# Cross attention with its value products issued once per group of four heads, and the second query tile's transposed scores divided by heads

## The chip, the core and the metric

The kernel runs on one core of one Trainium2 chip. The metric is the device time of one execution, in microseconds (us). The runs of the kernel before took 505.22, 505.7 and 510.95 us (median 505.7). The execution that the profiler recorded took 508.26 us, with a span of 506.4 us between its first and last instruction.

## What is computed

Four batches of 256 tokens with 256 channels pass through a gated cross attention and then a gated transformer block (self attention with 16 heads of 128, then four experts). The change touches only the cross attention, which in the reference is, for 16 query heads of 16 channels and 4 key/value heads:

```python
q = _rms_norm(q, q_norm_w)          # q: 256 tokens x 256
k = _rms_norm(k, k_norm_w)          # k, v: 256 tokens x 64
# heads, then rotary position on q and k
qg = q.reshape(B, N_KV_HEADS, g, T, hd)         # 4 groups of g = 4 heads
scores = jnp.einsum('bgnqd,bgkd->bgnqk', qg, k) * scale
scores = jnp.where(causal, scores, -1e+30)
attn = jax.nn.softmax(scores, axis=-1)
out = jnp.einsum('bgnqk,bgkd->bgnqd', attn, v)
return out.reshape(B, T, C) @ w_out.T
```

## The kernel before

**Cross attention.** A batch has 256 queries in two tiles of 128 and 256 keys in two tiles of 128. Work goes by group `m` of four heads that share one key head: 4 batches x 4 groups = 16 groups. Each group has three pieces, and piece `p = 3m + z` runs through a software pipeline of 53 steps (`for p in range(NPX + VLAG)`, with NPX = 48 and VLAG = 5). `k` is the step's number within a batch, 0 to 11. In step `p` TensorE does, in this order:

- `x_scores(p)` (L1102, matmuls L1112 and L1113): scores with queries on the partitions, in one of two PSUM banks `S_B`. It waits for `s_max` of piece p-2. VectorE takes the row maxima of them in `x_max` (L801, L810) into `nxm`.
- in some steps `q_turn` (L1069, eight transposes; ScalarE copies them out in `q_evac`, L477), `out_turn` (L1079) and `out_project` (L1090).
- `x_turned(p - 3)` (L1116): the same scores again with keys on the partitions, in a bank of `PT_B`, 512 columns a piece. Piece z = 0 is key tile 0 with query tile 0, z = 1 is key tile 0 with query tile 1, z = 2 is key tile 1 with query tile 1, each for all four heads. L1126 is the product, L1128 adds the causal mask where key and query tile are the same, and L1130 subtracts each head's row maximum by a matmul of 128 columns per head ("shift matmul": a column of `nxm` broadcast as weights, times the identity). ScalarE turns a piece into probabilities in `x_exp` (L495, L500), in one of four slots of `probs`.
- in some steps `norm_turn` (L1093, L1099), transposes of normed rows `nh` that VectorE makes in `residual` (L748, phases 0 to 5 in six steps, `nh` at L780).
- in steps p = 9, 12, ... `o_turn` (L1149, L1155), which transposes the group's outputs. VectorE divides them by the softmax sums in `norm_out` (L734, L742 and L744).
- `x_values(p - 5)` (L1134, L1145): probabilities times values, four matmuls of 128x32 weights, one for each head, each on 32 partitions of `bank[4]`. They take float32, and the trace has two records for each matmul. ScalarE copies the group's result to `oT` in `oT_evac` (L488, L493) after the third piece.

Each engine runs its instructions in the order in which they are written here. VectorE's step holds `x_max(p)`, then what the step has of `norm_q`, `hidden_t`, `norm_out`, `pack` (L707, copies L711 to L715) and `residual`. GpSimd makes the next batch's queries in `prep` (L319), then splits weights (L377 to L385), then `hidden_low` (L387). There are no loads from DRAM in the pipeline except two weight loads that SyncE starts near its end.

**After it** come a short stage that starts the self attention (`project_qk` and `project_v`, all at L1192), the self attention's loop, and the experts. Their code is the same in both kernels. The last `norm_turn` before them is that of batch 2 (L1184), and TensorE can't pass it before VectorE has written `nh`.

Of the kernel before, what the change touches and what calls it, by code (L numbers as in the profile page):

```python
# [12 lines left out]
ACT = mybir.ActivationFunctionType  # L13
AX = mybir.AxisListType

P = 128
# [4 lines left out]
XH, XG, XD = 16, 4, 16  # L21
XS = 8
XP = 12
VP = 32
TLAG, VLAG = 3, 5
# [22 lines left out]
def build_kernel(nc, x, ctx_in, cst, cols, rows, bv, wqkv, wo, w_out_t, w_gate, be2, we, out):  # L48
    with ExitStack() as stack:
        def sb(name, shape, dt=F32):  # L50
            return stack.enter_context(nc.sbuf_tensor(name, shape, dt))
# [45 lines left out]
        sm = sb("sm", [P, 2, 384])  # L97
        nm = sb("nm", [P, 2, 2])
        rs = sb("rs", [P, 2, 2])
        probs = sb("probs", [P, 4, 512])  # L100
        PR = probs[:, 0:2, :]
        PTs = probs[:, 2:4, :]
        o_parts = sb("o_parts", [P, 2, 1024], F32R)
# [21 lines left out]
        kT = yacc[:, :, :].rearrange("p t n -> p (t n)").bitcast(BF16).rearrange("p (b g n) -> p b g n", b=B, g=XG)  # L125
        qT = qk_room[:, :, :].rearrange("p a n -> p (a n)").bitcast(BF16).rearrange("p (x t h n) -> p x t h n", x=2, t=2, h=8)


        v_slots = room[:, 0:NT * XG * VP].rearrange("p (n d) -> p n d", d=VP)
# [6 lines left out]
        nxm = sb("nxm", [P, 3, 8], BF16)  # L136
# [11 lines left out]
        bank = [ps(f"bank{n}") for n in range(8)]  # L148
        S_B = bank[0:2]
        PT_B = bank[2:4]  # L150
# [4 lines left out]
        ident_bf = bf_sb[:, 0:P]  # L155
        mask_bf = bf_sb[:, P:2 * P]
# [9 lines left out]
        s = {n: sem(n) for n in names.split()}  # L166
# [11 lines left out]
            g, j = divmod(k, 3)  # L178
            return (g, 0, [4 * g + n for n in range(4)]) if j == 0 else (g, 1, [4 * g + 2 * (j - 1) + n for n in range(2)])

        def block_of(z):

            return ((0, 0), (0, 1), (1, 1))[z]


        M6, M7 = [("Q", 0, 0, 0), ("Q", 0, 0, 1)], [("K", b) for b in range(B)]
        for b in range(B):
# [274 lines left out]
        def _(act):  # L462
# [24 lines left out]

            def oT_evac(m):  # L488

                act.wait_ge(s["pv_pe"], 3 * m + 3)  # L490
                if m >= 2:
                    act.wait_ge(s["o_pe"], m - 1)
                act.activation(oT[:, m % 2, :], bank[4][:, 0:256], ACT.Copy).then_inc(s["oT_ready"], 1)  # L493

            def x_exp(p):  # L495

                act.wait_ge(s["st_pe"], p + 1)
                if p >= 4:
                    act.wait_ge(s["pv_pe"], p - 3)
                act.activation(probs[:, p % 4, :], PT_B[p % 2][:, :], ACT.Exp).then_inc(s["s_exp"], 1)  # L500

            q_evac(0, 0, 0)
            q_evac(0, 0, 1)
            for p in range(NPX + VLAG):
                b, k = divmod(p, XP)
# [92 lines left out]
            for n in range(2 * NE):  # L598
# [8 lines left out]
                c, m = divmod(n, NE)  # L607
# [439 lines left out]
        def _(pe):  # L1047
# [68 lines left out]
            def x_turned(p):  # L1116

                b, k = divmod(p, XP)
                m, z = divmod(p, 3)
                g, h = k // 3, 4 * (k // 3)  # L1120
                kt, t = block_of(z)
                pe.wait_ge(s["s_max"], 3 * m + (1 if z == 0 else 3))
                if p >= 2:
                    pe.wait_ge(s["s_exp"], p - 1)
                by_head = PT_B[p % 2][:, :].rearrange("p (h n) -> p h n", h=4)
                pe.matmul(by_head, kT[:, b, g, kt * P:(kt + 1) * P], qT[:, h // 8, t, h % 8:h % 8 + 4, :], start=True, stop=False)  # L1126
                if kt == t:
                    pe.matmul(by_head, mask_bf, ident_bf.unsqueeze(1).to_broadcast([P, 4, P]), start=False, stop=False)  # L1128
                for n in range(4):
                    ins = pe.matmul(PT_B[p % 2][:, n * P:(n + 1) * P], nxm[:, m % 3, 4 * t + n:4 * t + n + 1].to_broadcast([P, P]), ident_bf,  # L1130
                                    start=False, stop=(n == 3))
                ins.then_inc(s["st_pe"], 1)

            def x_values(p):  # L1134

                b, k = divmod(p, XP)
                m, z = divmod(p, 3)
                kt, t = block_of(z)
                pe.wait_ge(s["s_exp"], p + 1)
                if p == 0:  # L1140
                    pe.wait_ge(s["va_ready"], 1 + B)
                if z == 0 and m:
                    pe.wait_ge(s["oT_ready"], m)
                for n in range(4):
                    ins = pe.matmul(bank[4][32 * n:32 * (n + 1), t * P:(t + 1) * P], v_slots[:, XG * (2 * b + kt) + k // 3, :],  # L1145
                                    probs[:, p % 4, n * P:(n + 1) * P], start=(z != 2), stop=(z != 1))
                ins.then_inc(s["pv_pe"], 1)

            def o_turn(m):  # L1149
# [14 lines left out]
            for p in range(NPX + VLAG):  # L1164
                b, k = divmod(p, XP)
                if p < NPX:
                    x_scores(p)
                    if k in (3, 4):
                        q_turn(b, 1, k - 3)
                    if k == 8 and b:  # L1170
                        out_turn(b - 1)
                    if k == 9 and b:
                        out_project(b - 1)
                    if k in (9, 10) and b + 1 < B:
                        q_turn(b + 1, 0, k - 9)
                if TLAG <= p < NPX + TLAG:
                    x_turned(p - TLAG)
                if k == 5 and b >= 2:
                    norm_turn(b - 2)
                if p >= 9 and p % 3 == 0:  # L1180
                    o_turn((p - 9) // 3)
                if p >= VLAG:
                    x_values(p - VLAG)
            norm_turn(B - 2)  # L1184

            def three(outp, pairs):
# [260 lines left out]
```

## Time and profile before

| | before |
|---|---|
| runs | 505.22, 505.7, 510.95 us |
| profiled execution | 508.26 us, span 506.4 us |
| TensorE matmuls | 453.2 us busy, 89% of the span |
| VectorE | 367.1 us, 72% |
| ScalarE | 239.6 us, 47% |
| GpSimd | 232.8 us, 46% |

"PE" is TensorE's matmuls and "PEld" its weight loads, which overlap them. DVE is VectorE, ACT ScalarE, POOL GpSimd. Matmuls are pipelined, so a matmul's own duration (0.2 us and more) is longer than the time after which the next starts. What a matmul costs in a full stream is read from the distance between starts. The cross attention's pipeline lies from about 30 to 125 us of the span.

### The profile page before, as it was taken

How to read it: one execution, taken by the hardware profiler on the slowest of the kernel's cores; microseconds unless marked ns; L12 is line 12 of the kernel's file. 1: busy time of each engine (PE TensorE's matmuls, PEld its weight loads, DVE VectorE, ACT ScalarE, POOL GpSimd, SP SyncE). 2: the span in 40 equal slices, each digit the busy share in tenths (PEclk: the TensorE clock that was granted, in tenths of full speed). 3: DMA queues.
4: the chain of work that ended last, by engine and by line, in shares of the span. 5: the costliest groups of instructions: out<-in, count | busy, mean ns of one | idle time of the engine just before them, and what ended most of it. 6: DMA issues, size and time to landing. Idle time of an engine off the chain costs nothing.

```text
span 506.4 us, 10710 instructions
## 1 busy us (share of the span) xinstructions
PE 453.2 (89%) x3396; PEld 386.2 (76%) x3396; DVE 367.1 (72%) x1163; ACT 239.6 (47%) x613; POOL 232.8 (46%) x318
## 2 busy tenths in 40 slices
PE   0289998898777999999999999999999998689996
PEld 0166666675565899999999999999999997578895
DVE  5876669776557878788788887887877878835544
ACT  2026555453113555555655546556455565164342
POOL 5945709710345545446446445346454431162342
PEclk9999999999979999999999999999999998897899
DMA  8100000200123343352342532532533310000011
GB/s 286 28 3 1 2 1 3 84 1 1 23 62 84 72 119 84 84 145 64 78 133 58 143 85 62 145 74 52 144 83 83 77 29 0 2 0 2 0 43 42
DMA packets 19881, 31.41 MB, mean 62 GB/s; under 512 B 6020, under 2 KB 8200, under 8 KB 19848
## 3 DMA queue, kind: packets, MB, share of 16 engines
q1 hardware_dynamic: 15928, 22.31, 18.1%
q10 hardware_dynamic: 3920, 8.69, 5.7%
q8 instruction: 18, 0.29, 0.2%
q14 instruction: 15, 0.12, 0.1%
HBM read 13.16 MB, written 1.05 MB: 28 GB/s over the span
## 4 chain that ended last, share of the span: by engine, by line
PE 80%; DVE 12%; POOL 3%; issue 3%; DMA 1%; ACT 1%; ACTq 0%; DVEq 0%
PE bank L1192 42%; PE bank L1272 5%; PE bank L1235 5%; PE bank L1263 4%; PE bank L1145 3%; PE bank L1112 3%; PE bank L1273 3%; PE bank L1234 3%; PE bank L1126 2%; PE bank L1130 2%; PE bank L1090 1%; PE bank L1113 1%; PE bank L1128 1%; PE bank L1069 1%; DMA rows_sb<-in_rows 1%
## 5 line engine op out<-in xcount | busy, mean ns | idle before, releaser
L401 POOL TENSOR_TENSOR room<-room,qk_room 128x512 f32<-128x512 f32 x64 | 82.3, 1287 | 102.8 <-DMA qk_room<-qk_room 102.6
L542 ACT ACTIVATE probs<-sm,nm 128x128 f32<-128x128 f32 (+1 forms) x128 | 57.3, 448 | 116.2 <-DVE nm L917 116.2
L1192 PE MATMUL bank<-hH,qk_parts 128*128 128x512 f32 x256 | 81.0, 398 | 0.0
L840 DVE SCALAR_TENSOR_TENSOR qk_room<-bank,qk_bias,cst_sb 128x512 f32<-128x512 f32 x64 | 48.0, 750 | 37.2 <-PE bank L1192 35.8
L1192 PE MATMUL bank<-hL,qk_parts 128*128 128x512 f32 x128 | 62.4, 488 | 6.6 <-DVE room L840 5.7
L1192 PEld LDWEIGHTS bank<-hH,qk_parts 128*128 128x128 f32 x256 | 48.8, 191 | 10.1
L840 DVE SCALAR_TENSOR_TENSOR room<-bank,qk_bias,cst_sb 128x512 f32<-128x512 f32 x64 | 47.6, 743 | 0.0
L1192 PE MATMUL bank<-woH,o_parts 128*128 128x256 f32 x256 | 47.2, 283 | 0.0
L810 DVE TENSOR_REDUCE nxm<-bank 128x2 bf16<-128x512 f32 (+1 forms) x48 | 32.5, 688 | 14.9 <-PE bank L1113 14.3
L500 ACT ACTIVATE probs<-bank 128x512 f32<-128x512 f32 x48 | 28.6, 596 | 26.1 <-PE bank L1130 25.4
L1192 PE MATMUL bank<-woL,o_parts 128*128 128x256 f32 x128 | 39.0, 305 | 1.1 <-DVE o_parts L905 1.1
L1192 PEld LDWEIGHTS bank<-woH,o_parts 128*128 128x128 f32 x256 | 40.0, 192 | 0.0
L1272 PE MATMUL bank<-probs,V 128*128 128x256 f32 x128 | 39.0, 387 | 0.6 <-DVE o_parts L905 0.6
L1192 PE MATMUL bank<-wvL,hH 128*128 128x256 f32 x128 | 39.3, 307 | 0.0
L1235 PE MATMUL bank<-room 128*128 128x256 f32 x128 | 38.2, 380 | 0.0
L1192 PE MATMUL bank<-wvH,hH 128*128 128x256 f32 x128 | 36.4, 284 | 0.0
L450 POOL TENSOR_TENSOR qk_parts<-G,o_parts 128x512 fp32r<-128x512 f32 x16 | 20.7, 1298 | 34.0 <-ACT o_parts L616 33.5
L1192 PE MATMUL bank<-wvH,hL 128*128 128x256 f32 x128 | 36.3, 283 | 0.0
L1263 PE MATMUL bank<-cst_sb,probs 128*128 128x128 f32 x192 | 31.7, 274 | 4.9 <-DVE probs L961 4.9
L351 POOL TENSOR_TENSOR qk_parts<-stg,qk_parts 128x256 fp32r<-128x256 f32 x32 | 23.8, 743 | 26.5 <-ACT qk_parts L566 26.5
L556 ACT ACTIVATE o_parts<-bank,bv_pair 128x256 fp32r<-128x256 f32 x64 | 30.3, 474 | 11.6 <-PE bank L1273 10.8
L1263 PEld LDWEIGHTS bank<-cst_sb,probs 128*128 128x128 f32 x192 | 24.4, 140 | 14.6 <-DVE probs L961 6.8
(200 smaller groups left out, 1242.2 us busy)
## 6 DMA issues: line engine op xcount, KB each, us to landing
qk_room<-qk_room SPq DMA_DIRECT2D x128, 128.0 KB, 2.3
stg<-in_wqkv ACTq DMA_DIRECT2D x6, 768.0 KB, 4.6
stge<-in_we ACTq DMA_DIRECT2D x7, 256.0 KB, 3.2
stg<-in_wqkv SPq DMA_DIRECT2D x2, 768.0 KB, 6.4
stgo<-in_wo ACTq DMA_DIRECT2D x6, 256.0 KB, 3.6
x_sb<-in_x SPq DMA_DIRECT2D x4, 256.0 KB, 6.2
out_y<-yacc SPq DMA_DIRECT2D x4, 256.0 KB, 2.3
cst_sb<-in_cst SPq DMA_DIRECT2D x1, 520.0 KB, 6.9
```

What stands on the lines that cost most here:

```text
L351: pool.tensor_tensor(wqkL[:, c], stg[:, k, :, r * HD:(r + 1) * HD], wqkH[:, c].bitcast(F32), ALU.subtract).then_inc(s["wqk_ready"], 1)
L401: pool.tensor_tensor(v, v, qk_sw[:, q, :], ALU.subtract).then_inc(s["rope_done"], 1)
L450: pool.tensor_tensor(GL[:, (n // 2) % 2, n % 2, :], G[:, n % 2, :], GH[:, (n // 2) % 2, n % 2, :].bitcast(F32), ALU.subtract).then_inc(s[" ...
L500: act.activation(probs[:, p % 4, :], PT_B[p % 2][:, :], ACT.Exp).then_inc(s["s_exp"], 1)
L542: ins = act.activation(PR[:, q, a:e], sm[:, q, a:e], ACT.Exp, bias=nm[:, q, t:t + 1], scale=-1.0, accum_out=rs[:, q, t:t + 1])
L556: act.activation(oH[:, ((j - 2) // 2) % 2, q, :], bank[3][:, 0:256], ACT.Identity, bias=head_bias(j)).then_inc(s["b_oH"], 1)
L810: dve.tensor_reduce(nxm[:, m % 3, a:a + len(heads)], S_B[p % 2][:, :].rearrange("p (h n) -> p h n", h=len(heads)), AX.X, ALU.max, negate=T ...
L840: return dve.scalar_tensor_tensor(out.rearrange("p (b t) -> p b t", b=2), O_B[q][:, :].rearrange("p (b t) -> p b t", b=2), qk_bias[:, c:c ...
L1192: ins = pe.matmul(outp, l, r, start=(m == 0), stop=(m == n - 1))
L1235: pe.matmul(S_B[j % 2][:, P:3 * P], QT[:, 2 * r, second], QT[:, 2 * r + 1, both], start=True, stop=True).then_inc(s["b_s"], 1)
L1263: ins = pe.transpose(bank[2][:, n * P:(n + 1) * P], PR[:, 1 - q, n * P:(n + 1) * P], ident)
L1272: pe.matmul(bank[3][:, 0:256], V[:, 2 * b, r * HD:(r + 1) * HD], PTs[:, q, 0:256], start=True, stop=False)
```

## The change

The code of three functions and the storage of the probabilities change.

- `x_values` is called once per group, in steps p = 7, 10, 13, ... (`x_values((p - 7) // 3)`), and issues all twelve matmuls there. Before, four were issued in every step from p = 5. The group's third set of four was in the same step as the twelve are now. Its wait for the copy `oT_ready` of the group before moves with it, two steps later than before. `pv_pe` counts groups now, and `oT_evac` and `x_exp` wait accordingly.
- `probs` has six slots instead of four, three for each of two groups. `x_exp` waits for the values of two groups before.
- For the second query tile `x_turned` puts heads 0 and 1 with both key tiles into piece z = 1, heads 2 and 3 with both key tiles into piece z = 2. The product is two matmuls of 256 columns, the mask one of 256 columns, and a head's shift is one matmul of 2x128 columns that serves both key tiles. The columns of a group add up to 4096 before and after.

The core of the diff:

```diff
-        probs = sb("probs", [P, 4, 512])
+        probs = sb("probs", [P, 6, 512])
...
+        def prob_slot(m, z):
+
+            return probs[:, 3 * (m % 2) + z, :]
...
-                act.wait_ge(s["pv_pe"], 3 * m + 3)
+                act.wait_ge(s["pv_pe"], m + 1)
...
+                m, z = divmod(p, 3)
                 act.wait_ge(s["st_pe"], p + 1)
-                if p >= 4:
-                    act.wait_ge(s["pv_pe"], p - 3)
-                act.activation(probs[:, p % 4, :], PT_B[p % 2][:, :], ACT.Exp).then_inc(s["s_exp"], 1)
+                if m >= 2:
+                    act.wait_ge(s["pv_pe"], m - 1)
+                act.activation(prob_slot(m, z), PT_B[p % 2][:, :], ACT.Exp).then_inc(s["s_exp"], 1)
...
-                pe.wait_ge(s["s_max"], 3 * m + (1 if z == 0 else 3))
+                pe.wait_ge(s["s_max"], p + 1)
...
+                else:
+                    by_keys = PT_B[p % 2][:, :].rearrange("p (k h n) -> p k h n", k=2, h=2)
+                    first = 2 * (z - 1)
+                    for kt in range(2):
+                        pe.matmul(by_keys[:, kt, :, :], kT[:, b, g, kt * P:(kt + 1) * P],
+                                  qT[:, h // 8, 1, h % 8 + first:h % 8 + first + 2, :], start=(kt == 0), stop=False)
+                    pe.matmul(by_keys[:, 1, :, :], mask_bf, ident_bf.unsqueeze(1).to_broadcast([P, 2, P]), start=False, stop=False)
+                    for n in range(2):
+                        ins = pe.matmul(by_keys[:, :, n, :], nxm[:, m % 3, 4 + first + n:5 + first + n].to_broadcast([P, P]),
+                                        ident_bf.unsqueeze(1).to_broadcast([P, 2, P]), start=False, stop=(n == 1))
...
-                if z == 0 and m:
+                else:
                     pe.wait_ge(s["oT_ready"], m)
-                for n in range(4):
-                    ins = pe.matmul(bank[4][32 * n:32 * (n + 1), t * P:(t + 1) * P], v_slots[:, XG * (2 * b + kt) + k // 3, :],
-                                    probs[:, p % 4, n * P:(n + 1) * P], start=(z != 2), stop=(z != 1))
+                for kt, t in ((0, 0), (0, 1), (1, 1)):
+                    for n in range(4):
+                        z, c = (0, n) if t == 0 else (1 + n // 2, 2 * kt + n % 2)
+                        ins = pe.matmul(bank[4][32 * n:32 * (n + 1), t * P:(t + 1) * P], v_slots[:, XG * (2 * b + kt) + g, :],
+                                        prob_slot(m, z)[:, c * P:(c + 1) * P], start=(kt == 0), stop=(kt == t))
...
-                if p >= VLAG:
-                    x_values(p - VLAG)
+                if p >= 7 and p % 3 == 1:
+                    x_values((p - 7) // 3)
```

TensorE's order in step 22 (k = 10 of batch 1), from the second `q_turn` of that pair to the first scores of step 23. L1145 is the value product, L1126 and L1130 the transposed scores and their shift. Before:

```order
L1069 MATMUL bank<-bf_sb,q_room 128x128 [waits m6_free,qpack_ready]
L1069 MATMUL bank<-bf_sb,q_room 128x128 x7
L1126 MATMUL bank<-qk_room,yacc 128x512 [waits s_exp,s_max]
L1130 MATMUL bank<-bf_sb,nxm 128x128 x4
L1145 MATMUL bank<-probs,room 32x128 [waits s_exp]
L1145 MATMUL bank<-probs,room 32x128 x3
L1112 MATMUL bank<-yacc,qk_room 128x256 [waits s_max,m6_free]
```

The same place of the change, where the value product is L1153 and the second tile's transposed scores L1134 to L1138:

```order
L1069 MATMUL bank<-bf_sb,q_room 128x128 [waits m6_free,qpack_ready]
L1069 MATMUL bank<-bf_sb,q_room 128x128 x7
L1134 MATMUL bank<-qk_room,yacc 128x256 [waits s_exp,s_max]
L1134 MATMUL bank<-qk_room,yacc 128x256
L1136 MATMUL bank<-bf_sb 128x256
L1138 MATMUL bank<-bf_sb,nxm 128x2x128 x2
L1153 MATMUL bank<-probs,room 32x128 [waits oT_ready,s_exp]
L1153 MATMUL bank<-probs,room 32x128 x11
L1112 MATMUL bank<-yacc,qk_room 128x256 [waits s_max,m6_free]
```

Twelve value products stand where four stood, and the wait for `oT_ready` is here now.

TensorE's order in step 23, the next one. Before:

```order
L1126 MATMUL bank<-qk_room,yacc 128x512 [waits s_exp,s_max]
L1128 MATMUL bank<-bf_sb 128x512
L1130 MATMUL bank<-bf_sb,nxm 128x128 x4
L1145 MATMUL bank<-probs,room 32x128 [waits oT_ready,s_exp]
L1145 MATMUL bank<-probs,room 32x128 x3
L1112 MATMUL bank<-yacc,qk_room 128x128 [waits s_max,m7_free,m6_free]
```

The change:

```order
L1134 MATMUL bank<-qk_room,yacc 128x256 [waits s_exp,s_max]
L1134 MATMUL bank<-qk_room,yacc 128x256
L1136 MATMUL bank<-bf_sb 128x256
L1138 MATMUL bank<-bf_sb,nxm 128x2x128 x2
L1112 MATMUL bank<-yacc,qk_room 128x128 [waits s_max,m7_free,m6_free]
```

No value product and no wait for `oT_ready` is left in this step, nor in step 24 behind `o_turn`.

## Rows read from the trace of the kernel before

**Rows 1.** Page, part 1: busy us, share of the span, instructions.
```profile
PE 453.2 (89%) x3396; PEld 386.2 (76%) x3396; DVE 367.1 (72%) x1163; ACT 239.6 (47%) x613; POOL 232.8 (46%) x318
```
**Rows 2.** By stretch: length, busy us of PE, PEld, DVE, ACT, POOL; clock, DMA.
```profile
43.00:70.00 27.00, 26.83 (x353) 18.64 (x352) 15.76 (x38) 15.61 (x26) 12.18 (x26) 1.00 0.01 2
70.26:83.40 13.14, 11.69 (x156) 7.76 (x155) 12.59 (x39) 7.12 (x13) 7.15 (x17) 1.00 0.01 1
83.40:95.10 11.70, 11.59 (x137) 8.18 (x135) 7.96 (x20) 6.42 (x12) 11.12 (x22) 1.00 0.06 12
95.10:107.40 12.30, 10.69 (x146) 7.18 (x146) 11.78 (x36) 6.52 (x11) 2.79 (x3) 1.00 0.22 79
107.40:116.40 9.00, 9.00 (x104) 6.39 (x101) 4.57 (x12) 3.67 (x7) 2.50 (x2) 1.00 0.00 0
```
**Rows 3.** Timeline of TensorE, steps 24 to 26: start us, us, instruction, count.
```profile
72.21 0.39 PE L1130 MATMUL bank<-bf_sb,nxm 128*128 128x128 bf16 x4
72.43 0.39 PE L1155 MATMUL bank<-cst_sb,V 128*128 128x128 f32 x2
...
75.11 0.39 PE L1130 MATMUL bank<-bf_sb,nxm 128*128 128x128 bf16 x4
75.43 0.43 PE L1145 MATMUL bank<-probs,room 128*32 128x128 f32 x8
75.79 0.23 PE L1112 MATMUL bank<-yacc,qk_room 128*128 128x128 bf16 x1
```
**Rows 4.** Timeline of TensorE at the end of the pipeline.
```profile
122.34 0.64 PE L1145 MATMUL bank<-probs,room 128*32 128x128 f32 x16
124.98 0.66 PE L1099 MATMUL bank<-cst_sb,nh 128*128 128x128 f32 x4 [2.00 <-DVE nh L780]
```
**Rows 5.** Timeline of ScalarE and TensorE, steps 21 to 23.
```profile
66.91 1.02 ACT L477 ACTIVATE qk_room<-bank 128x1024 bf16<-128x1024 bf16 x1 [2.54 <-PE bank L1069]
68.38 0.61 PE L1069 MATMUL bank<-bf_sb,q_room 128*128 128x128 bf16 x8
70.43 0.39 ACT L493 ACTIVATE V<-bank 128x256 f32<-128x256 f32 x1
70.49 0.39 PE L1130 MATMUL bank<-bf_sb,nxm 128*128 128x128 bf16 x4
70.96 0.43 PE L1145 MATMUL bank<-probs,room 128*32 128x128 f32 x8
```
**Rows 6.** Timeline of VectorE: idle time and its releaser in brackets.
```profile
70.26 0.69 DVE L810 TENSOR_REDUCE nxm<-bank 128x2 bf16<-128x512 f32 x1 [0.33 <-PE bank L1113]
...
83.83 0.69 DVE L810 TENSOR_REDUCE nxm<-bank 128x4 bf16<-128x512 f32 x1 [0.46 <-PE bank L1113]
...
95.44 1.31 DVE L712 COPY q_room<-q_room 128x256 bf16<-128x256 bf16 x1
...
108.10 0.69 DVE L810 TENSOR_REDUCE nxm<-bank 128x4 bf16<-128x512 f32 x1 [0.70 <-PE bank L1113]
```
**Rows 7.** TensorE's waits for VectorE within the pipeline.
```profile
82.22 0.66 PE L1099 MATMUL bank<-cst_sb,nh 128*128 128x128 f32 x4 [1.37 <-DVE nh L780]
...
100.06 0.27 PE L1112 MATMUL bank<-yacc,qk_room 128*128 128x256 bf16 x1 [1.51 <-DVE nxm L810]
```
**Rows 8.** Timeline of GpSimd: start and end of its chain.
```profile
75.66 0.73 POOL L329 TENSOR_TENSOR G<-qn,WC 128x256 f32<-128x256 f32 x1 [11.53 <-DVE qn L681]
...
96.61 1.28 POOL L394 TENSOR_TENSOR yacc<-yacc,rows_sb 128x512 f32<-128x512 f32 x1
```
**Rows 9.** Timeline of TensorE behind the pipeline: its longest waits.
```profile
135.18 0.50 PE L1192 MATMUL bank<-hL,qk_parts 128*128 128x512 f32 x1 [2.12 <-DVE room L840]
...
141.08 0.79 PE L1192 MATMUL bank<-hL,qk_parts 128*128 128x512 f32 x1 [2.81 <-DVE room L840]
```
**Rows 10.** Busy us by stretch behind the pipeline, columns as in rows 2.
```profile
142.00:144.00 2.00, 2.00 (x6) 1.41 (x6) 0.00 (x0) 0.00 (x0) 0.61 (x1) 0.50 0.35 79
...
146.00:148.00 2.00, 1.31 (x7) 1.11 (x6) 2.00 (x5) 1.23 (x2) 1.24 (x2) 0.74 0.05 11
```

More of the change, by code:

```diff
@@ L179, in piece @@
             return (g, 0, [4 * g + n for n in range(4)]) if j == 0 else (g, 1, [4 * g + 2 * (j - 1) + n for n in range(2)])
-        def block_of(z):
-            return ((0, 0), (0, 1), (1, 1))[z]
+        def prob_slot(m, z):
+            return probs[:, 3 * (m % 2) + z, :]
         M6, M7 = [("Q", 0, 0, 0), ("Q", 0, 0, 1)], [("K", b) for b in range(B)]
@@ L1120, in x_turned @@
                 g, h = k // 3, 4 * (k // 3)
-                kt, t = block_of(z)
-                pe.wait_ge(s["s_max"], 3 * m + (1 if z == 0 else 3))
+                pe.wait_ge(s["s_max"], p + 1)
                 if p >= 2:
                     pe.wait_ge(s["s_exp"], p - 1)
-                by_head = PT_B[p % 2][:, :].rearrange("p (h n) -> p h n", h=4)
-                pe.matmul(by_head, kT[:, b, g, kt * P:(kt + 1) * P], qT[:, h // 8, t, h % 8:h % 8 + 4, :], start=True, stop=False)
-                if kt == t:
+                if z == 0:
+                    by_head = PT_B[p % 2][:, :].rearrange("p (h n) -> p h n", h=4)
+                    pe.matmul(by_head, kT[:, b, g, 0:P], qT[:, h // 8, 0, h % 8:h % 8 + 4, :], start=True, stop=False)
@@ L1128, in x_turned @@
                     pe.matmul(by_head, mask_bf, ident_bf.unsqueeze(1).to_broadcast([P, 4, P]), start=False, stop=False)
-                for n in range(4):
-                    ins = pe.matmul(PT_B[p % 2][:, n * P:(n + 1) * P], nxm[:, m % 3, 4 * t + n:4 * t + n + 1].to_broadcast([P, P]), ident_bf,
-                                    start=False, stop=(n == 3))
-                ins.then_inc(s["st_pe"], 1)
[L1134 to L1140, printed above, removed]
+                    for n in range(4):
+                        ins = pe.matmul(by_head[:, n, :], nxm[:, m % 3, n:n + 1].to_broadcast([P, P]), ident_bf, start=False, stop=(n == 3))
+                else:
[8 more added lines that the diff above has]
+                                        ident_bf.unsqueeze(1).to_broadcast([P, 2, P]), start=False, stop=(n == 1))
@@ L1141, in x_values @@
+                ins.then_inc(s["st_pe"], 1)
+            def x_values(m):
+                b, g = divmod(m, XG)
+                pe.wait_ge(s["s_exp"], 3 * m + 3)
+                if m == 0:
                     pe.wait_ge(s["va_ready"], 1 + B)
-                if z == 0 and m:
+                else:
                     pe.wait_ge(s["oT_ready"], m)
-                for n in range(4):
-                    ins = pe.matmul(bank[4][32 * n:32 * (n + 1), t * P:(t + 1) * P], v_slots[:, XG * (2 * b + kt) + k // 3, :],
-                                    probs[:, p % 4, n * P:(n + 1) * P], start=(z != 2), stop=(z != 1))
+                for kt, t in ((0, 0), (0, 1), (1, 1)):
+                    for n in range(4):
+                        z, c = (0, n) if t == 0 else (1 + n // 2, 2 * kt + n % 2)
+                        ins = pe.matmul(bank[4][32 * n:32 * (n + 1), t * P:(t + 1) * P], v_slots[:, XG * (2 * b + kt) + g, :],
+                                        prob_slot(m, z)[:, c * P:(c + 1) * P], start=(kt == 0), stop=(kt == t))
```

## The prediction

> **What bounds the kernel now.** The page's busy times come first [rows 1]: TensorE has 89% of the span, the next engine 72%. Only the cross attention's pipeline changes, about 30 to 125 us, so I read that part by stretches [rows 2]. The reader should see two kinds. From 43 to 70 us and from 107.4 to 116.4 us TensorE is busy 26.8 of 27.0 and 9.0 of 9.0 us, with VectorE at 58% and 51%: there TensorE sets the pace. From 70.3 to 83.4 and from 95.1 to 107.4 us VectorE is busy 12.6 of 13.1 and 11.8 of 12.3 us, and TensorE has gaps. Then VectorE sets the pace. The timeline of TensorE shows those gaps [rows 7]: 1.37 us at 82.22 for `nh` (step 29) and 1.51 us at 100.06 for a row maximum (step 38). What TensorE saves in a stretch of the second kind makes such a gap longer, and nothing else.
>
> **The value products.** A set of four costs more than its matmuls, because the array changes from 128-column to 32-column weights and back. Four shift matmuls take 0.22 us when something with full width follows (72.21 to 72.43), but L1145 starts 0.32 us after them (75.11 to 75.43), and full width resumes 0.36 us after that (75.79) [rows 3]. So a set takes 0.10 + 0.36 = 0.46 us; the printed starts are rounded, and I take 0.455. The profile has one place with two sets back to back [rows 4]: 16 records in 0.64 us, against 8 records in 0.43 us [rows 3]. A further set behind the first costs 0.21 to 0.22 us. Twelve products in a row then cost 0.455 + 2 x 0.215 = 0.885 us, where three sets cost 1.365 us. That saves 0.48 us a group, and with starts printed to 0.01 us it may be 0.46 to 0.50. I use 0.47, so 16 x 0.47 = 7.5 us of TensorE time in all.
>
> The bounds of that: if the switch went away and nothing else did, the saving would be two times (0.10 + 0.36 - 0.215), the same 0.49. If a run of twelve behaved like three separate sets, it would be 0. The back-to-back row is the same operation with the same operands, so I stay by it.
>
> The Trainium skill (TensorE: Matmul & The Clock Gate, the section on packing small matmuls) states that a weight load overlaps running matmuls only when it goes to another row group. All twelve products use all rows, so by that rule they would not overlap. The row with 16 records does not agree with it.
>
> **The transposed scores.** The columns stay 4096 a group. Two products of 256 columns stand for one of 512, and four shifts of 2x128 for eight of 128; matmuls per group go from 17 to 16 there. Starts follow each other by columns: 128 columns take 0.055 us (four in 0.22 [rows 3]). I take the sum as nothing. A fixed cost of some ns a matmul would change it by under 0.02 us a group either way, 0.3 us in all; nothing in the trace has the two-part 2x128 output, and if it wrote at half rate the four shifts would cost 0.43 us more a group, 7 us in all. The existing scores and mask matmuls already read the identity repeatedly over heads and run at full rate, so I give that little weight. The earlier wait (`s_max` of p rather than of the whole group) gains nothing: two pieces later has been reduced before `x_scores` of the same step could pass.
>
> **Waits that move.** In step 23 L1145 waits for `oT_ready` [rows 5]: the shifts end their slot at 70.71, the switch would allow 70.81, it starts at 70.96, because ScalarE's copy L493 ran until 70.82. That is 0.15 us, in steps 11, 17, 23 and 35, where ScalarE is late by its 1.02 us `q_evac`. The change asks for that copy two steps later, so this goes. But the value set between the two `q_turn` of a pair goes too. The second one starts at 68.38 and needs `q_evac`, done at 67.93. With 0.455 us less ahead of it it would come at 67.93 plus nothing, and the hand-over takes 0.14 us (70.82 to 70.96), so it waits 0.15 us. Behind it only other pairs wait on ScalarE. Gains and losses of this kind are equal within 0.2 us.
>
> The six `probs` slots cost nothing: `x_exp` of group m waits for the values of m-2, issued two steps earlier. The twelve products ask for `x_exp` of a piece turned two steps earlier, as the last set does now. ScalarE at 15.6 of 27 us [rows 2] has room.
>
> **What reaches the end.** I follow the saving through the stretches.
>
> 1. Up to step 23 TensorE leads: six groups, 6 x 0.47 = 2.8 us. Waits for `oT_ready` in steps 11 and 17 give 0.3, three `q_turn` pairs (steps 9, 15, 21) take 0.45. Sum 2.65 us.
> 2. From step 23 VectorE is continuously occupied from 70.26 until the maxima that end at 83.4, with 0.46 us idle before step 30 [rows 6]. Its work doesn't change, so this whole stretch moves by 2.65 us. TensorE's two groups in it (0.9 us) lengthen the 1.37 us gap to some 2.3 us.
> 3. Steps 30 to 35 let TensorE lead again, and it gains about 0.9 us. But GpSimd's chain runs from 75.66 to 97.89 without a stop [rows 8], started by `norm_q` inside the VectorE stretch. So it moves by 2.65 us only. VectorE's copies in step 35 take 1.31 us each while GpSimd's operations of 1.28 us run [rows 6, 8], and end with them. Step 36 therefore moves by 2.65 us too. The 1.51 us gap becomes about 2.45 us.
> 4. From step 39 to step 51 TensorE leads (VectorE is idle 0.70 us before 108.10 [rows 6], and TensorE has no gap in 107.4 to 116.4 [rows 2]): four groups, 1.9 us, less 0.15 for one `q_turn` pair. 1.75 us.
> 5. The last wait, 2.00 us for `nh` at 124.98 [rows 4], hangs on `norm_out` of step 51, which TensorE's `o_turn` releases. It moves along. The twelve products of the last group lie in this wait, and what follows is relative to it.
>
> Sum: 2.65 + 1.75 = 4.4 us. On the profiled execution's own time, 508.26 us, that is 503.9. That execution lies 2.6 us above the median of the runs, 505.7 us; against the median it is **501.3 us**, -0.9%.
>
> **Rivals.**
>
> - *The gaps shrink instead of growing, and nearly all of it counts.* VectorE's stretches hold waits that GpSimd causes (the copies of 1.31 us), and another alignment could spare some. Bound: 7.5 us and 0.6 of `oT_ready` waits, 8.1, so 497.6 us. Against it: VectorE was busy 12.6 of 13.1 us. Chance 0.12.
> - *VectorE or ScalarE bind sooner.* VectorE's slack in step 30 is 0.46 us and in step 42 0.70 us. If also the stretches 1 and 4 lose half, 2.2 us are left: 503.5 us. Chance 0.17.
> - *Other side: the longer gaps drop TensorE's clock.* After the wait of 2.12 us the clock stayed, after that of 2.81 us [rows 9] it was at 0.50, the level of 1.2 GHz, through 142 to 144 us and still 0.74 on average in 146 to 148 us [rows 10]: 5 us or more at half, so 2.5 to 3.4 us of work lost. The new gaps, 2.3 and 2.45 us, lie between the two. One drop gives 501.3 + 3 = 504.3 us. It turns the sign with two: 507.3 us. Against it: the 2.00 us gap at 124.98 was harmless. Chance of one 0.09, of two 0.02.
> - *The products don't run together.* If each of the six rounds of a group waited for its weights (so that the 0.215 us which two rounds of a further set take became the time of one), twelve would take 6 x 0.215 + 0.30 = 1.59 us, 0.22 more than now; with ten groups that count, +2.2 us and 507.9. This is what the skill's rule named above would do. Chance 0.02, since the row with 16 records contradicts it. That a run of twelve costs three sets, 505.7 us, and that the shift matmuls run at half rate (4.3 us back over the ten groups that count, 505.6 us), get 0.04 together.
>
> **How the numbers follow.** The forecast has the remaining 0.54, with 500 to 502.7 as its own range (rounding of the 0.47 us by 0.02 over ten groups, 0.2; the hand-over waits, 0.5; the spread of 0.5 us between the two lower runs). The range 498.0 to 505.0 us leaves out the full saving below and the cases with no gain above. A measurement of this kernel can tell about 2% from no change, 10 us. Faster by over 2% would need under 495.6 us, more than TensorE saves in all: 0.03. Slower by over 2%: 0.02. Within: 0.95.
>
> **What would show it.** In the profile after: 24 records of the value product in about 0.85 us; the gap before `norm_turn` in step 29 near 2.3 us and that in step 38 near 2.45 us; no idle time before VectorE's maximum of step 30; the last `norm_turn` of the pipeline near 120.6 instead of 124.98 us. I am wrong if 24 records take over 1.1 us, if the shifts' starts are more than 0.12 us apart, or if that last `norm_turn` comes at 117 or at 123 us. A different time with `norm_turn` as forecast would lie in the clock behind it.

## The result, and the profile after

The changed kernel takes 501.71 us (median of 20 runs, 498.78 to 506.44), the kernel before 506.56 us (20 runs, 503.2 to 510.95). The ratio is 0.9912 with a 95% interval of 0.9891 to 0.9932, so 4.5 us less (3.4 to 5.5). It is clear of noise and under 2%. The forecast was 501.3 us.

Part 1 of the page after (busy us, share of the span of 501.4 us, instructions):

```profile
PE 446.8 (89%) x3365; PEld 391.0 (78%) x3380; DVE 366.6 (73%) x1163; ACT 240.2 (48%) x613; POOL 232.9 (46%) x318
```

VectorE, ScalarE and GpSimd do what they did [rows 1]. TensorE is busy 6.4 us less.

The timeline of TensorE, steps 24 to 26 of the kernel after (start us, us, instruction, count, idle time before it in brackets), answers to [rows 3]:

```profile
69.41 0.38 PE L1138 MATMUL bank<-bf_sb,nxm 128*128 128x256 bf16 x2
69.72 0.86 PE L1153 MATMUL bank<-probs,room 128*32 128x128 f32 x24
70.52 0.28 PE L1112 MATMUL bank<-yacc,qk_room 128*128 128x256 bf16 x1
...
71.18 0.38 PE L1138 MATMUL bank<-bf_sb,nxm 128*128 128x256 bf16 x2
71.85 0.22 PE L1112 MATMUL bank<-yacc,qk_room 128*128 128x128 bf16 x1 [0.28 <-DVE nxm L810]
```

Twelve products are 24 records in 0.86 us, and full width resumes 0.80 us after they begin. Two shift matmuls of 2x128 columns take 0.31 us here with the switch behind them (69.41 to 69.72). Where full width follows, ahead of the scores of step 12 of the same kernel, they take 0.22 us:

```profile
46.98 0.38 PE L1138 MATMUL bank<-bf_sb,nxm 128*128 128x256 bf16 x2
47.20 0.22 PE L1112 MATMUL bank<-yacc,qk_room 128*128 128x128 bf16 x1
```

TensorE's waits in the pipeline of the kernel after, answering to [rows 7] and the last of [rows 4]:

```profile
74.10 0.27 PE L1112 MATMUL bank<-yacc,qk_room 128*128 128x256 bf16 x1 [0.32 <-ACT qk_room L476]
79.05 0.65 PE L1099 MATMUL bank<-cst_sb,nh 128*128 128x128 f32 x4 [1.69 <-DVE nh L780]
...
97.03 0.27 PE L1112 MATMUL bank<-yacc,qk_room 128*128 128x256 bf16 x1 [1.31 <-DVE nxm L810]
98.62 0.22 PE L1112 MATMUL bank<-yacc,qk_room 128*128 128x128 bf16 x1 [0.55 <-DVE nxm L810]
...
120.22 0.66 PE L1099 MATMUL bank<-cst_sb,nh 128*128 128x128 f32 x4 [1.32 <-DVE nh L780]
```

The same three points were at 82.22, 100.06 and 124.98 us [rows 7, 4]. They moved by 3.17, 3.03 and 4.76 us. Between the first and the second nothing was gained, though TensorE had three groups' saving there. The rest of the kernel kept its length: 506.4 - 124.98 = 381.4 us before and 501.4 - 120.22 = 381.2 us after.

The stretch that VectorE fills, and two stretches behind the first gap (length, busy us of PE, PEld, DVE, ACT, POOL, then granted clock, DMA share, GB/s), answering to [rows 2]:

```profile
67.08:80.30 13.22, 10.79 (x147) 8.35 (x149) 12.59 (x39) 6.69 (x12) 7.23 (x17) 1.00 0.00 1
81.00:82.00 1.00, 1.00 (x8) 0.81 (x7) 0.97 (x3) 0.60 (x1) 0.92 (x2) 0.50 0.08 25
83.00:84.00 1.00, 1.00 (x18) 0.71 (x20) 1.00 (x5) 0.64 (x2) 0.87 (x3) 0.50 0.00 0
```

VectorE's 12.59 us are the 12.59 us of before [rows 2], and TensorE is busy 0.9 us less in it. Behind the gap TensorE's granted clock is at 0.50, the level of 1.2 GHz, from 80.7 to 84.1 us.

### The profile page after: what moved, and what is told of

The parts are those of the page before. It is cut to its first block, busy times and chain, and to the rows that moved or that the text cites. A ratio compares the mean times of both kernels' runs of the same rounds, so it can differ in the third digit from the quotient of the medians.

```text
span 501.4 us, 10661 instructions
## 1 busy us (share of the span) xinstructions
PE 446.8 (89%) x3365; PEld 391.0 (78%) x3380; DVE 366.6 (73%) x1163; ACT 240.2 (48%) x613; POOL 232.9 (46%) x318
## 4 chain that ended last, share of the span: by engine, by line
PE 78%; DVE 14%; POOL 3%; issue 3%; DMA 1%; ACT 1%; ACTq 0%; DVEq 0%
PE bank L1200 42%; PE bank L1280 5%; PE bank L1243 5%; PE bank L1271 4%; PE bank L1242 3%; PE bank L1281 3%; PE bank L1112 2%; PE bank L1153 2%; DVE nxm L810 2%; PE bank L1090 1%; PE bank L1113 1%; PE bank L1069 1%; DMA rows_sb<-in_rows 1%; PE bank L1134 1%; PE bank L1127 1%
```

## The experiments

**How they are compared.** The code behind the pipeline is the same everywhere, yet in these profiles it takes 374.4 to 381.4 us, with its half-clock stretches in different places. So beside the ratios I compare the pipeline itself, from its first L1112 to the last `norm_turn` before the self attention, in each profile: 95.4 us in the kernel before (29.61 to 124.98) and 90.5 us in the kernel after (29.75 to 120.22).

Two things blur that column by 1 to 2 us. One is the start. The first value product stands in step 5, and in these profiles the scores of step 5 come 6.2 to 8.4 us after the first ones (8.33 in the kernel before, 7.63 in the change). The last column leaves this start out. It is too long where the start was early, because TensorE then stands for VectorE ahead of the scores of step 9: 1.1 us in e5, e7 and e10, 0.6 us or less in e3, e4, e6 and e9, nothing elsewhere. The other is a stretch at the granted clock of 0.50, which lies within the pipeline in the change, e1, e3, e5, e7, e8 and e11. Steps 39 to 42 take 6.95 us with it in e1 and e5, against 5.46 us in the change, and 7.35 us in e3, against 5.79 us in the kernel before. So it costs some 1.5 us there.

| run | time, us | ratio to before, 95% | pipeline, us | from step 5, us |
|---|---|---|---|---|
| before | 505.5 to 506.6 | 1 | 95.4 | 87.0 |
| the change | 501.71 | 0.9912 (0.9891 to 0.9932) | 90.5 | 82.8 |
| e1_values_only | 500.83 | 0.9879 (0.9844 to 0.9914) | 92.7 | 84.3 |
| e2_heads_only | 511.18 | 1.0086 (1.0042 to 1.013) | 97.2 | 90.9 |
| e12_heads_four_strips | 506.54 | 1.0008 (0.998 to 1.0036) | 94.3 | 87.1 |
| e3_three_sets | 505.08 | 1.0002 (0.9967 to 1.0037) | 95.4 | 88.8 |
| e4_before_light | 499.11 | 0.9867 (0.9836 to 0.9898) | 90.3 | 84.1 |
| e5_after_light | 496.64 | 0.9792 (0.975 to 0.9833) | 88.2 | 81.9 |
| e11_before_light_early | 499.5 | 0.9847 (0.9808 to 0.9886) | 90.5 | 83.7 |
| e10_after_light_early | 492.71 | 0.9724 (0.9686 to 0.9761) | 84.6 | 78.3 |
| e6_spread | 501.75 | 0.9908 (0.9872 to 0.9945) | 90.3 | 83.1 |
| e7_values_first | 503.19 | 0.9941 (0.9915 to 0.9967) | 92.0 | 85.4 |
| e8_weights_early | 502.18 | 0.9905 (0.9872 to 0.9938) | 90.9 | 83.3 |
| e9_weights_earlier | 500.16 | 0.9888 (0.9866 to 0.991) | 89.0 | 81.8 |

### Which part of the change carries it

**Grouped value products alone.** The change with the old transposed scores.

```diff
-                        z, c = (0, n) if t == 0 else (1 + n // 2, 2 * kt + n % 2)
+                        z, c = kt + t, n
```

> Only the value products are grouped (twelve in one step, six slots for the probabilities); the transposed scores keep their four heads per piece. Theory (the saving is that of the array's switches): TensorE saves the same 0.47 us a group, so 4.4 us less than before (-0.9%), the same as the whole change within 0.3 us. Rival (the division by heads carries part of the gain, through fewer and longer shift matmuls): under 2.5 us less than before.

The ratio is 0.9879, 6.1 us less (4.4 to 7.9), and its interval overlaps that of the change. So the grouping carries the gain. Whether the two are equal within the 0.3 us expected is finer than the runs can tell. The pipeline in the profile is 2.2 us longer than the change's: 0.8 us of that is the start, and 1.5 us is a half clock behind a gap of 2.37 us in step 38:

```profile
97.81 0.27 PE L1112 MATMUL bank<-yacc,qk_room 128*128 128x256 bf16 x1 [2.37 <-DVE nxm L810]
...
100.00:102.00 2.00, 1.78 (x14) 1.45 (x14) 1.52 (x5) 0.81 (x1) 0.00 (x0) 0.50 0.00 0
```

**Division by heads alone.** The first attempt gave each piece its own set: piece 1 the products of heads 0 and 1 for both key tiles.

```diff
+                for kt, t, n in ([(0, 0, n) for n in range(4)] if z == 0 else
+                                 [(kt, 1, 2 * (z - 1) + n) for kt in range(2) for n in range(2)]):
```

> Only the transposed scores are divided by heads; the value products stay in three sets of four in three steps (the sets of the second query tile are two heads with both key tiles). Theory: the same time as before within 0.5 us, since 48 switches stay and the columns are equal. Rival (division carries part of the gain): 2 us or more less. Rival (the two-part output of 2x128 columns is slow): 2 us or more longer.

It takes 0.86% longer (0.4 to 1.3), 4.4 us, so by the letter the theory fell. The timeline of TensorE shows a cause that isn't the division. A set that uses two column strips for two products each takes longer than one that uses four strips once:

```profile
60.62 0.38 PE L1138 MATMUL bank<-bf_sb,nxm 128*128 128x256 bf16 x2
60.93 0.63 PE L1154 MATMUL bank<-probs,room 128*32 128x128 f32 x8
61.49 0.28 PE L1112 MATMUL bank<-yacc,qk_room 128*128 128x256 bf16 x1
...
62.92 0.43 PE L1154 MATMUL bank<-probs,room 128*32 128x128 f32 x8
```

0.63 us against 0.43 us for the same eight records, as two sets in a row cost [rows 4]. Two such sets a group are 0.4 us, 6.4 us over 16 groups. Part of it falls where VectorE leads: the waits of step 29 and step 38 are 0.81 and 0.56 us here. The next run takes this away: each set has all four strips, and the second and third wait for the whole group's probabilities.

```diff
+                pe.wait_ge(s["s_exp"], p + 1 if z == 0 else 3 * m + 3)
...
+                kt, t = ((0, 0), (0, 1), (1, 1))[z]
+                for n in range(4):
+                    slot, c = (0, n) if t == 0 else (1 + n // 2, 2 * kt + n % 2)
```

> Only the transposed scores divided by heads, as in the run e2_heads_only, but each of the three sets of value products uses all four column strips (the second and third wait for the whole group's probabilities). Theory (e2 was longer because its sets used two strips twice, four rounds instead of two): the same as before within 1 us. Rival (the division itself costs, by shift matmuls with 2x128 columns): 3 us or more longer than before, as e2.

The ratio is 1.0008 (0.998 to 1.0036, or 1.0 us less to 1.8 us more), and from step 5 the pipeline takes 87.1 us, the kernel before 87.0 us. The division costs nothing and brings nothing by itself that these show, and its two-part shift matmuls run at full rate. But it needs the grouping: with one set per piece it would cost what e2 shows.

**The switches or the moved waits.** All of the change, with full-width matmuls between its three sets.

```diff
+                if p >= 7 and p % 3 == 1:
+                    x_values((p - 7) // 3, 0)
                 if p < NPX:
                     x_scores(p)
+                if p >= 7 and p % 3 == 1:
+                    x_values((p - 7) // 3, 1)
...
-                    x_values((p - 7) // 3)
+                    x_values((p - 7) // 3, 2)
```

> The change, but its twelve products stand as three sets of four in one step: ahead of the scores, behind them, and behind the transposed scores, so full-width matmuls lie between. Same waits moved as in the change, 48 switches as before. Theory (switches): the gain is gone but for waits, 505 to 506 us where before is 505.7, and the set takes 0.45 us of TensorE again. Rival (the gain comes from asking later for probabilities and for the copy of the outputs, not from the switches): 4 us less than before, as the change.

The ratio is 1.0002 (1.7 us less to 1.9 us more). The pipeline is 95.4 us, as before, but that the two agree to 0.1 us is chance. This profile holds a half clock, and the kernel before holds a slow start:

```profile
100.00:103.00 3.00, 2.77 (x22) 2.44 (x24) 2.06 (x7) 1.12 (x2) 0.00 (x0) 0.50 0.00 0
```

Less some 1.6 us for that stretch it would be 93.8 us, an estimate, and the fair partner is e12 with 94.3 us. So the moved waits are worth at most about 0.5 us in the trace. The gain is in the main the 32 pairs of switches that are gone, not the later wait for probabilities or for `oT`.

### Where the saving is absorbed

Both kernels with less work on VectorE. They leave out the refinement of the reciprocal root for batches 0 and 1, and for batches 2 and 3 four of the five copies that repeat parts of the queries, so their outputs are not the reference's:

```diff
-                if 3 <= phase <= 5:
+                if 3 <= phase <= 5 and b == 2:
                     rsqrt_step(h, y, w, 4)
...
+                if b < 2:
                     dve.tensor_copy(v[:, :, 1, :], v[:, :, 0, :])
                     dve.tensor_copy(v[:, :, 2, :], v[:, :, 0, :])
                     dve.tensor_copy(v[:, :, 4, :], v[:, :, 3, :])
                     dve.tensor_copy(v[:, :, 5, :], v[:, :, 3, :])
```

> The kernel before with less VectorE work in the pipeline; leaves out the reciprocal root's refinement for batches 0 and 1 (9 small operations each) and four of the five copies that repeat the queries' parts for batches 2 and 3. Theory (VectorE sets the pace in two stretches of before): the two gaps of 1.37 and 1.51 us go, 2.5 to 3.5 us less than before, 502.7 us.

> The change with the same VectorE work left out as in the light kernel before: the refinement for batches 0 and 1 and four of five copies for batches 2 and 3. Theory (the change's TensorE saving is absorbed where VectorE sets the pace): with that work gone nearly all 15 groups ahead of the last wait count, 6 to 7 us less than the light kernel before, instead of 4.4 to 4.9. Rival (what the change gains is independent of VectorE's load): 4.4 to 4.9 us less than the light kernel before.

The light kernel before gains more than expected, 6.7 us by the ratio (5.2 to 8.3). Its two gaps are gone, and from step 5 on its pipeline is 2.9 us shorter, as expected. The profile is also shorter by 2.1 us ahead of step 5 and by 5.1 us behind the pipeline (376.3 us), places that the edit doesn't touch, and I can't assign the rest of the gain in the runs. The light change is 3.8 us below it by the ratios and 2.1 us by the pipelines, with a half clock of some 1.5 us in the latter. That is no more than without the edit, so the theory as put fell: VectorE's own work was not all that absorbs. The timeline of the light change (TensorE, VectorE and GpSimd apart) shows what is left ahead of the scores of step 39, and its granted clock behind:

```profile
94.25 0.22 PE L1113 MATMUL bank<-yacc,qk_room 128*128 128x128 bf16 x1 [2.39 <-DVE nxm L811]
...
91.03 1.06 DVE L768 TENSOR_SCALAR small<-mv 128x2 f32<-128x2 f32 x1
92.00 0.15 DVE L769 TENSOR_SCALAR small<-mv 128x2 f32<-128x2 f32 x1
92.19 1.12 DVE L631 TENSOR_SCALAR small<-small 128x4 int32<-128x4 int32 x1
...
90.79 1.27 POOL L390 TENSOR_TENSOR hL<-sm,hH 128x512 fp32r<-128x512 f32 x1
92.02 1.26 POOL L393 TENSOR_TENSOR yacc<-yacc,rows_sb 128x512 f32<-128x512 f32 x1
...
95.00:98.00 3.00, 3.00 (x21) 2.27 (x20) 1.19 (x4) 1.62 (x2) 0.00 (x0) 0.50 0.00 0
```

VectorE's operations on 2 and 4 columns take 1.06 and 1.12 us and end when GpSimd's do (92.06 and 93.28). Their neighbour takes 0.15 us. By this reading GpSimd's chain, started by `norm_q` in step 25, holds VectorE until it ends. So the next pair of runs also moves the weight splitting of that chain into GpSimd's idle time ahead of batch 3:

```diff
+            pool.wait_ge(s["d_wqkv"], 16)
+            pool.wait_ge(s["d_cols"], 16)
+            for c in range(4):
...
+            low_o(0)
             prep(3, 0)
```

> The kernel before with the same two edits: lighter VectorE (leaves out the refinement for batches 0 and 1 and four of five copies for batches 2 and 3) and GpSimd's weight splitting early. Theory: little under the light kernel before, whose two gaps were gone already: within 1 us of its 499 us.

> The change with VectorE's work lighter (leaves out the refinement for batches 0 and 1 and four of five copies for batches 2 and 3) and GpSimd's weight splitting moved early as well. Theory: both of the things that absorb are gone, TensorE leads up to the last wait, and this is 6 to 7.5 us less than the kernel before with the same two edits. Rival (something else absorbs, ScalarE or the last VectorE chain): 4 to 5 us less than it.

The kernel before stays at 499.5 us, the change goes to 492.71 us. They differ by 6.8 us (6.2 us by the ratios, 5.9 us by the pipelines), against 4.5 us in the real kernels. With both absorbers gone TensorE is never idle by these stretches of the change, the second from the place that held the second gap. Between them one wait of 0.43 us is left:

```profile
71.21 0.22 PE L1113 MATMUL bank<-yacc,qk_room 128*128 128x128 bf16 x1 [0.43 <-DVE nxm L811]
...
46.41:65.75 19.34, 19.34 (x269) 15.57 (x267) 11.50 (x29) 12.14 (x20) 14.90 (x34) 1.00 0.01 2
...
88.00:96.00 8.00, 8.00 (x119) 6.49 (x120) 6.87 (x23) 5.19 (x8) 0.00 (x0) 1.00 0.01 3
97.00:107.00 10.00, 10.00 (x128) 8.16 (x126) 6.21 (x14) 4.92 (x9) 2.50 (x2) 1.00 0.02 3
```

So TensorE's full saving is 6 to 7 us. In the real kernels 4.5 us of it show by the ratios, and 3.8 to 4.2 us by the pipelines (94.3 us in e12, whose start is 0.4 us shorter than the change's, less 90.5; or 87.0 less 82.8 from step 5). A quarter to a third is absorbed by VectorE's work together with GpSimd's chain. The intervals of the ratios alone leave room for nothing to a half: by an estimate from them the full saving is 3.5 to 9.0 us. It is the traces, with the gaps gone, that show the absorption.

### Attempts to get the absorbed part back

**Weight splitting ahead of batch 3**, with nothing left out.

> The change with GpSimd's splitting of the first weights (8.4 us, the rows from wqkH to woL) moved ahead of prep of batch 3, into the 11.5 us in which GpSimd is idle there. Theory (the second gap, before the scores of step 38, is held by the end of GpSimd's chain, because VectorE's copies and small operations wait for each of its operations): VectorE's copies in step 35 take 0.2 us again, the gap of 1.31 us shrinks below 0.5 us, and 1.5 to 3 us less than the change, 499 to 500 us. Rival (VectorE's own work fills that stretch): under 0.7 us less.

VectorE's copy, 1.31 us before [rows 6], is short again, and the gap of step 38 is gone. But new waits stand in steps 26, 27 and 33 (1.27 us at 87.52), and the granted clock is at 0.50 from 73.6 to 77.0 us. In steps 26 and 27 GpSimd's operations now meet VectorE's full stretch:

```profile
94.72 0.22 DVE L712 COPY q_room<-q_room 128x256 bf16<-128x256 bf16 x1
...
71.96 0.27 PE L1112 MATMUL bank<-yacc,qk_room 128*128 128x256 bf16 x1 [1.44 <-DVE nxm L810]
73.55 0.26 PE L1112 MATMUL bank<-yacc,qk_room 128*128 128x128 bf16 x1 [0.55 <-DVE nxm L810]
```

The ratio is 0.9905, that of the change. The mechanism was right and the gain was given back in another stretch.

**Weight splitting ahead of batch 2**, where VectorE is less busy: the same block in front of `prep(2, 0)`.

> The change with GpSimd's weight splitting (8.4 us) moved two batches earlier, ahead of prep of batch 2, where VectorE is busy 58% and GpSimd idle for 7.8 us. Theory (GpSimd's operations hold VectorE's, and where VectorE has slack that costs nothing): the gap before the scores of step 38 is gone as in e8_weights_early, and step 26 has no new wait of 1.4 us as there; the last norm_turn of the pipeline 1.0 to 2.0 us nearer to the pipeline's start than in the change, 500 us. Rival (the gap goes and another wait takes its place, as in e8): no less than the change.

```profile
53.06 0.27 PE L1112 MATMUL bank<-yacc,qk_room 128*128 128x256 bf16 x1 [0.33 <-DVE nxm L810]
61.49 0.22 PE L1112 MATMUL bank<-yacc,qk_room 128*128 128x128 bf16 x1 [0.75 <-DVE nxm L810]
...
79.89 0.66 PE L1099 MATMUL bank<-cst_sb,nh 128*128 128x128 f32 x4 [1.68 <-DVE nh L780]
...
96.72 0.22 PE L1112 MATMUL bank<-yacc,qk_room 128*128 128x128 bf16 x1 [0.28 <-DVE nxm L810]
118.32 0.66 PE L1099 MATMUL bank<-cst_sb,nh 128*128 128x128 f32 x4 [1.31 <-DVE nh L780]
```

The first gap stays as in the change, the second is gone, and the last `norm_turn` comes at 118.32 us in a pipeline that began at 29.36: 1.5 us less. (From step 5 it is 1.1 us, since this start was 0.4 us earlier; by step 9 the two are level.) That is a balance. Two waits for a maximum are new, in steps 16 and 21. VectorE's `norm_q` takes 1.84 us beside GpSimd, in the change 0.73 us, and GpSimd's `prep` with the copies of VectorE behind it comes later:

```profile
50.47 1.84 DVE L681 TENSOR_SCALAR qn<-x_sb,mv,small 128x256 f32<-128x256 f32 x2
...
59.02 0.23 DVE L711 COPY q_room<-q_room 128x256 bf16<-128x256 bf16 x1 [0.80 <-POOL q_room L341]
```

The scores of step 23 come 38.05 us after the first, in the change 36.79. So the moved work costs 1.26 us there, and some 2.8 us come back at step 38. The runs give 500.16 us and 0.9888; the interval overlaps the change's, so the runs alone don't settle 1.5 us. Of the complete kernels this one has the shortest pipeline and the lowest median, though e1's ratio, 0.9879, is a little lower.

**VectorE's `residual` spread out** over more steps.

```diff
+                spread = {0: 0, 2: 1, 4: 2, 5: 3, 6: 4, 7: 5} if b1 < B - 2 else {n: n for n in range(6)}
...
-                if k == 5 and b >= 2:
+                if k == 7 and b >= 2:
                     norm_turn(b - 2)
```

> The change, with VectorE's residual of batches 0 and 1 spread over steps 10, 0, 2, 4, 5, 6 and 7 instead of six steps in a row with the busiest ones among them, norm_turn and hidden_t two steps later. Nothing is left out. Theory (VectorE's two full stretches cost what the gaps show, some 1.7 and 1.9 us): 1.5 to 3 us less than the change, 499 to 500 us. Rival (GpSimd's chain or the copies in step 11 hold VectorE anyway): the first gap goes, the second stays, under 1 us less.

The ratio is 0.9908, no gain over the change, nearer to the rival than to the theory. The first gap is down to 0.99 us, but `out_project` now waits 0.89 us for the bank that `hidden_t` empties later, and steps 38 and 39 wait as before:

```profile
80.00 0.66 PE L1100 MATMUL bank<-cst_sb,nh 128*128 128x128 f32 x4 [0.99 <-DVE nh L780]
...
84.61 1.97 PE L1091 MATMUL bank<-w_out_sb,onT 128*128 128x256 f32 x8 [0.89 <-DVE sm L785]
95.58 0.27 PE L1113 MATMUL bank<-yacc,qk_room 128*128 128x256 bf16 x1 [1.43 <-DVE nxm L810]
97.69 0.22 PE L1113 MATMUL bank<-yacc,qk_room 128*128 128x128 bf16 x1 [1.07 <-DVE nxm L810]
```

**Value products ahead of `q_turn`.**

```diff
                     x_scores(p)
+                if p >= 7 and p % 3 == 1:
+                    x_values((p - 7) // 3)
+                if p < NPX:
                     if k in (3, 4):
```

> The change with the twelve products moved ahead of q_turn and of the transposed scores in their step. Theory (the change leaves 0.15 us waits of the second q_turn of each pair for ScalarE's q_evac): those waits go, seven pairs, of which four or five in stretches where TensorE leads: 0.5 to 0.8 us less than the change. Rival (the waits only move to another hand-over with ScalarE): the same as the change within 0.3 us.

A miss: 0.9941, some 1.5 us more than the change by the point values, though the intervals touch. From the scores of step 12 to those of step 23, with two `q_turn` pairs between, it takes 19.04 us (46.92 to 65.96) where the change takes 19.34 (47.20 to 66.54). That is the expected 0.15 us a pair. But the saving ends in a gap of 2.30 us in step 38, with a half clock behind it:

```profile
96.27 0.27 PE L1112 MATMUL bank<-yacc,qk_room 128*128 128x256 bf16 x1 [2.30 <-DVE nxm L810]
...
98.00:100.00 2.00, 1.78 (x17) 1.72 (x17) 1.86 (x6) 0.24 (x1) 0.00 (x0) 0.50 0.00 0
```

The pipeline is 1.5 us longer than the change's. At step 45, behind the half clock, it is 0.5 us behind the change. The rest comes in the last steps, where one `o_turn` waits for ScalarE's copy:

```profile
118.60 0.44 PE L1163 MATMUL bank<-cst_sb,V 128*128 128x128 f32 x2 [0.42 <-ACT V L492]
```

Why the runs are longer is argued from this one profile, not shown.

## Why the prediction was right, point by point

- **The saving per group, 0.47 us.** Confirmed. Twelve products are 0.86 us of records (forecast 0.85) and their set costs 0.09 + 0.80 = 0.89 us (forecast 0.885): 69.41 to 69.72 less two shifts at 0.22, then 69.72 to 70.52. The back-to-back row of the kernel before [rows 4] was the right basis. e3, with the switches back, loses the gain. The Trainium skill's rule that weight loads overlap running matmuls only across row groups (TensorE: Matmul & The Clock Gate, Part 3 on packing small matmuls) does not describe these products: with one row group for all of them, each further set of eight records adds 0.21 to 0.22 us (0.43, 0.64 and 0.86 us for 8, 16 and 24).
- **The transposed scores, nothing.** Confirmed by e12 (1.0008) and by the shifts' rate.
- **The moved waits, equal.** The waits for `oT_ready` are gone, and the `q_turn` wait of 0.15 us is there, as the 0.30 us that e7 takes away from two pairs shows. By e3 their sum is at most about 0.5 us.
- **Step 1, 2.65 us until VectorE leads.** The trace gives 3.17 us at the first gap, and the sizes agree once the start is allowed for. The pipeline began 0.14 us later, and TensorE came to full rate earlier in this execution, at a granted clock of 1.00 in both. The same eight transposes start at 36.32 us and take 1.06 us before, against:

```profile
36.38 0.61 PE L1069 MATMUL bank<-bf_sb,q_room 128*128 128x128 bf16 x8
37.37 0.27 PE L1112 MATMUL bank<-yacc,qk_room 128*128 128x256 bf16 x1
```

  The next scores start 0.99 us after them, in the kernel before 1.62 us after them:

```profile
36.32 1.06 PE L1069 MATMUL bank<-bf_sb,q_room 128*128 128x128 bf16 x8
37.94 0.27 PE L1112 MATMUL bank<-yacc,qk_room 128*128 128x256 bf16 x1
```

  3.17 + 0.14 - 0.63 = 2.68 us. The other profiles bear this out: from step 5 the kernel before needs 87.0 us and e12 87.1 us, though their starts differ by 1.1 us.
- **Steps 2 and 3, absorbed.** Confirmed in sum: the second point moved by 3.03 us, no more than the first. The place was off. I put 2.3 us in the gap of step 29; it was 1.69 us, with 0.28 us at 71.85 for a maximum and 0.32 us at 74.10 for ScalarE's copy of the queries, together 2.29 us. Before VectorE's maximum of step 30 it still had 0.19 us idle, where I had said none. The gap of step 38 was to be 2.45 us and was 1.31 us, with 0.55 us behind it. TensorE came late to it, since its clock was at 0.50 from 80.7 to 84.1 us. In e1, with the clock at 1.00 up to there, that gap was 2.37 us, as forecast.
- **What holds step 36.** I named GpSimd's chain, and that VectorE's copies end with its operations. e5 and e8 show it: with less work on VectorE the wait stayed, with GpSimd's work elsewhere it went.
- **Step 4, 1.75 us.** 4.76 - 3.03 = 1.73 us.
- **The rivals.** The clock rival came true in the profiled execution, once, and had 0.09. Its price of 3 us was too high, because the half clock lay in front of a point that GpSimd's chain holds anyway: from the scores of step 23 to those of step 39 the change takes 32.08 us with it and e1 31.93 us without. The gap was 1.69 us, below the 2.12 us that I had taken as harmless. The stretch at 0.50 was also shorter, 80.7 to 84.1 us, than the one I had priced it by, 140.2 to 147.0 us in the kernel before. The bounds between which I placed it were not bounds: e12 and e11 have the half clock at the very wait of 2.00 us that was harmless in the kernel before.

```profile
124.07 1.12 PE L1099 MATMUL bank<-cst_sb,nh 128*128 128x128 f32 x4 [2.00 <-DVE nh L780]
...
124.00:127.00 3.00, 2.93 (x9) 2.55 (x10) 1.07 (x4) 0.62 (x1) 0.00 (x0) 0.50 0.00 0
```

- **How close, and how much of it is luck.** The mechanism was right: a saving per group, counted only where TensorE leads. That 4.4 us meets 4.5 us to 0.1 us is luck, as the interval is 3.4 to 5.5 us, the pipelines give 3.8 to 4.2 us, and the half clock happened to fall where it cost nothing.

## What to carry to other kernels

When small column-tiled matmuls alternate with full-width ones, count the switches: here one costs 0.25 us a pair beside the matmuls, and a run of twelve takes 0.89 us where three runs of four take 1.36. Spread each set over all column strips, since two strips used twice cost 0.2 us more than four used once. Then follow the saving through each stretch to the engine that leads there, and through that engine to what holds it: what was absorbed here hung on VectorE's work and on a third engine's chain together, and taking VectorE's work away alone did not free it.

## What was not expected of the hardware

- The granted clock fell to 0.50 at gaps that had looked safe: 1.69 us in the change, 1.43 us in e3, 1.44 us in e8, 1.32 us in e6 (at 120.02), 2.30 us in e7, 2.37 us in e1 and 2.39 us in e5. A gap of 1.68 us in e9 had no half clock before 130 us, nor had the gaps of 1.37 and 1.51 us in the kernel before. The same gap as in the change, for the same instruction, had none in e1. The length of the gap alone does not decide it in these traces.

```profile
79.97 0.66 PE L1099 MATMUL bank<-cst_sb,nh 128*128 128x128 f32 x4 [1.69 <-DVE nh L780]
...
80.00:98.00 18.00, 15.10 (x199) 11.77 (x203) 14.17 (x33) 8.67 (x15) 14.98 (x28) 1.00 0.18 61
```

- VectorE's smallest operations (2 or 4 columns, 0.15 us) take over 1 us beside GpSimd's operations on 512 float32 columns, and so do its bf16 copies (1.31 us against 0.22 us). The lever is where the two meet. Moved into a stretch in which VectorE is less busy, the same GpSimd work cost TensorE 1.26 us there in e9 and gave back some 2.8 us; moved ahead of batch 3, in e8, it gave nothing.
- Identical code behind the pipeline took 374.4 to 381.4 us from one profile to another. That spread is as large as the change, so a saving of 1.5 us as in e9 is read from the stage in the trace, and the runs neither confirm nor deny it. The start of the pipeline varies as well, by 2.2 us up to the scores of step 5, ahead of all value products. A difference of whole pipelines is therefore read from a step behind the start.
